# Layer normalisation moved from a block of its own into the block of each cross attention

## The chip, the cores and the metric

The kernel runs on one core of a Trainium2 chip. The core has a matmul engine (TensorE, PE in the rows; PEld is its weight load), VectorE (DVE), ScalarE (ACT), GpSimd (POOL) and SyncE (SP, which issues DMAs). They run independent instruction streams and meet through semaphores. The metric is device time in microseconds (us), the median of several runs; lower is better.

## The reference

Two decoder layers over x, which has 8 batches of 128 tokens with 128 columns, in float32. Each layer is a self attention, a cross attention on a context of 77 rows per batch, and a mixture of experts, each behind a layer normalisation without gain or offset:

```python
x = x + L0_attn(_layernorm(x), ...)
x = x + L0_xattn(_layernorm(x), ctx_768, Wq, bq, Wk, bk, Wv, bv, Wo, bo)
x = x + L0_ffn(_layernorm(x), ...)
x = x + L1_attn(_layernorm(x), ...)
x = x + L1_xattn(_layernorm(x), ctx_768, Wq, bq, Wk, bk, Wv, bv, Wo, bo)
x = x + L1_ffn(_layernorm(x), ...)

def _layernorm(x, eps=1e-05):
    m = mean(x, -1); v = var(x, -1)
    return (x - m) / sqrt(v + eps)

def xattn(x, y, ...):             # 16 heads of 8 columns, 77 keys per batch
    q, k, v = x @ Wq + bq, y @ Wk + bk, y @ Wv + bv
    weights = softmax(einsum('bhqd,bhkd->bhqk', q, k) * 8 ** -0.5)
    return einsum('bhqk,bhkd->bqhd', weights, v) @ Wo + bo
```

## The kernel before

All 1024 tokens stay in on-chip memory for the whole kernel. `x_all` holds the residual stream (partition = token, 8 batches beside one another), `xn_all` its normalised copy, and `xnT_all` the transposed normalised copy (partition = column, 1024 tokens along the free side), which is what the products with weights read.

The program is a chain of stages. Each stage is a block: every engine gets its part of the block, and at its end all engines meet before the next block starts. In order: set-up, attention of layer 0, `layer_norm("n1_")`, `cross_attention(0)`, `mixture0`, `attention1` (which calls `layer_norm("n3_")` inside), `layer_norm("n4_")`, and `mixture1`, which first calls `cross_attention(1, loads)` and then runs its experts. The change touches the norms n1 and n4 and both cross attentions. The first is called the first place here, the second the second place.

`layer_norm` runs in two halves of four batches. VectorE takes the statistics of a half (L165, L168, L170), GpSimd raises the variance to the power -1/2 (L180), and after the statistics of both halves VectorE writes the eight batches of `xn_all` (L173). TensorE transposes each batch into PSUM (L185), and ScalarE copies each half, 128x512, to `xnT_all` (L190). The block ends there.

`cross_attention` starts with the query product: two float32 matmuls of 512 tokens each (L666), one for each half of `xnT_all`, into the two banks `sbk[0]` and `sbk[1]`, and ScalarE takes each out to `q` with the bias (L740). Meanwhile ScalarE loads its table for the exponential (L737), VectorE clears a PSUM bank (L774), and GpSimd adds the output bias to `x_all` (L823), which is first needed when a batch's output is added to `x_all` (L790), seven steps later. TensorE waits for both `q_out` and then starts 16 steps n, two for each batch. A step has four heads in two groups: scores (L688, in `sbk[n % 2]`), row maximum and shift (layer 0: a clamp L782, the maximum L799 on VectorE, the shift L829 on GpSimd; layer 1: L785 and L803 on VectorE), exponential (L769, ScalarE), eight transposes of the probabilities (L722), their copy to `pT` (L764, ScalarE), and sixteen small products with the values (L712). Each engine walks through the steps in a fixed order written out by hand, with lags between the parts. The normalisation for the following mixture is already done inside the steps, batch by batch.

`cross_attention(1, loads)` also has SP issue the loads of the first two experts of the second mixture (L1481 to L1487).

Of the kernel before, what the change touches and what calls it, by code (L numbers as in the profile page):

```python
# [18 lines left out]
ACT = mybir.ActivationFunctionType  # L19
# [3 lines left out]
B = 8  # L23
# [68 lines left out]
def program(nc, a, out, scratch, spread0):  # L92
# [17 lines left out]
    xnT_all = sb("xnT_all", [P, T])  # L110
# [70 lines left out]

    def norm_tensor(pe, n, turned):
        for b in range(B):
            pe.wait_ge(normed, B * n + b + 1)
            pe.transpose(turned[b // 4][:, P * (b % 4):P * (b % 4) + P], xn_all[:, b, :], ident).then_inc(turn_done, 1)  # L185

    def norm_scalar(act, n, turned):
        for j in range(2):
            act.wait_ge(turn_done, B * n + 4 * j + 4)
            act.activation(xnT_all[:, 512 * j:512 * j + 512], turned[j][:, :], ACT.Copy).then_inc(copied, 1)  # L190

    def layer_norm(tag, loads=None):

        with ExitStack() as st:
            _, ps, _ = tools(st, tag)
            turned = [ps(f"turned{j}") for j in range(2)]
            norms[0] += 1
# [24 lines left out]
    def setup_and_bias(bias0, w0):  # L222

        wq, wkv, wo = w0
        with ExitStack() as st:
# [50 lines left out]
            def _(act):  # L276
# [9 lines left out]
                for l in range(2):  # L286
                    for j in range(2):
# [6 lines left out]
                               ACT.Copy).then_inc(bias_out, 1)  # L294
                norm_scalar(act, 0, p_k[2:4])

            @block.tensor
            def _(pe):
# [12 lines left out]
                pe.wait_ge(k_out, 4)  # L311
                norm_tensor(pe, 0, p_k[2:4])

# [298 lines left out]
    def cross_attention(l, loads=None):  # L612
# [5 lines left out]
        with ExitStack() as st:  # L618
# [13 lines left out]
            bk = ps("back", (P, 4 * P))  # L632
            back = bk[:, :].rearrange("p (h c) -> p h c", c=32)
            SPARE = HG * NKV
            names = ("q_done", "q_out", "scores_done", "scores_read", "max_done", "shifted", "exp_done", "turn_done",
# [28 lines left out]
            def _(pe):  # L664
                for j in range(2):
                    pe.matmul(sbk[j][:, 0, :], wqx[l][:, :], xnT_all[:, 512 * j:512 * j + 512], start=True,  # L666
                              stop=True).then_inc(S["q_done"], 1)
                pe.wait_ge(S["q_out"], since["q_out"] + 2)
                pe.wait_ge(S["pv_zeroed"], since["pv_zeroed"] + 1)
                for n in range(2 * SLOTS + 5):  # L670
# [11 lines left out]
                    if n < STEPS:  # L682
                        b = n // 2
                        if n >= 2:
                            pe.wait_ge(S[bank_read], since[bank_read] + n - 1)
                        for u in range(2):
                            at = 32 * (2 * (n % 2) + u)
                            mm = pe.matmul(sbk[n % 2][:, u, 0:HG * NKV], q[at:at + 32, P * b:P * b + P],  # L688
                                           kblk[l][at:at + 32, b, :], start=True, stop=True)
# [46 lines left out]
            def _(act):  # L736
                act.preload_act_table(ACT.Exp)  # L737
                for j in range(2):
                    act.wait_ge(S["q_done"], since["q_done"] + j + 1)
                    act.activation(q[:, 512 * j:512 * j + 512], sbk[j][:, 0, :], ACT.Identity,  # L740
# [31 lines left out]
            @block.vector  # L772
            def _(dve):
                dve.memset(ob[:, :], 0.0).then_inc(S["pv_zeroed"], 1)  # L774
                for n in range(2 * B + 8):
# [45 lines left out]
            @block.gpsimd  # L821
            def _(pool):
                pool.tensor_tensor(x_all[:, :, :], x_all[:, :, :], free(bo, [[0, B], [1, P]]),  # L823
                                   ALU.add).then_inc(S["with_bias"], 1)
# [26 lines left out]
    with ctx:  # L851
        with ExitStack() as early:
# [4 lines left out]
            attention0(bias0, w0)  # L857
        layer_norm("n1_")
        cross_attention(0)
        mixture0(nc, tools, spread0, x_all, xnT_all, consts, tables, we_hi, we_lo, we_split)  # L860
        attention1(nc, a, tools, layer_norm, x_all, xn_all, xnT_all, consts, rows, cols, eps_pow)
        layer_norm("n4_")
        mixture1(nc, a, tools, cross_attention, x_all, xn_all, xnT_all, consts, tables)
# [964 lines left out]
```

## Time and profile before

| what | us |
|---|---|
| median of the three runs shown | 656.82 (656.30, 656.82, 679.62) |
| span of the profiled execution, first to last instruction | 631.4 |

The profile records one execution. Its times are microseconds from the first instruction of the span. The granted clock of TensorE is given as a share of full speed: 1.00 is 2.4 GHz, 0.50 is 1.2 GHz. In a timeline, instructions of a kind on one engine that follow one another closely are merged into one row with their count, so a row with a count gives the start of the first and the length of the whole run; the bracket gives the idle time of the engine ahead of it and who ended it.

### The profile page before, as it was taken

To read this page: it belongs to the slowest core of one execution; us is meant where nothing else is said; L and a number is where in the kernel's file an instruction comes from. 1 tells how busy PE (TensorE), PEld (TensorE's weight loads), DVE (VectorE), ACT (ScalarE), POOL (GpSimd) and SP (SyncE) were. 2 spreads that over 40 slices of the span, in tenths; PEclk is the share of its full clock that TensorE was granted. 3 is DMA by queue.
4 is the path that set the end of the run, shared out by engine and by line. 5 is a ranking of instruction groups with operands and counts; after the bars stand their busy time and mean duration, and the time that the engine had idled before them with its cause. 6 is when DMAs were issued, how large, how long until landed. Compare 5 with 4: busy or idle time off the path is not lost. (4 is left out here: it accounts for less than half of the span.)

```text
span 631.4 us, 9987 instructions
## 1 busy us (share of the span) xinstructions
PE 533.0 (84%) x3281; PEld 413.8 (66%) x3281; DVE 374.3 (59%) x875; ACT 326.1 (52%) x573; POOL 206.7 (33%) x229
## 2 busy tenths in 40 slices
PE   4698999989866998589999699864499967999996
PEld 2488898978853665457887387724266645777774
DVE  3376584756643465356666417765536638788875
ACT  3265454645403566435555326530246636788893
POOL 1688600000013346216655173011200255445510
PEclk9899999999876699789999569978559978899998
DMA  6913100000000000024432100000200001111201
GB/s 182 214 56 88 50 0 0 0 0 1 1 0 1 1 2 1 1 84 134 135 120 66 50 2 2 0 1 1 67 1 1 3 1 34 33 35 42 59 0 33
DMA packets 23412, 23.71 MB, mean 38 GB/s; under 512 B 3358, under 2 KB 17648, under 8 KB 23152
## 3 DMA queue, kind: packets, MB, share of 16 engines
q1 hardware_dynamic: 22528, 22.66, 12.5%
q10 hardware_dynamic: 848, 0.60, 0.3%
q8 instruction: 20, 0.33, 0.2%
q14 instruction: 16, 0.13, 0.1%
HBM read 22.64 MB, written 0.61 MB: 37 GB/s over the span
## 5 line engine op out<-in xcount | busy, mean ns | idle before, releaser
L1775 DVE TENSOR_TENSOR e_h_lo<-e_h,e_h_hi 128x512 fp32r<-128x512 f32 x60 | 50.7, 875 | 15.5 <-ACT e_h_hi L1636 15.4
L1045 POOL TENSOR_TENSOR e_gc<-e_g,e_c 128x512 f32<-128x512 f32 x32 | 42.0, 1314 | 42.0 <-ACT e_g L1028 22.4
L180 POOL TENSOR_TENSOR rstd<-var,eps_pow 128x4 f32<-128x4 f32 x8 | 8.3, 1039 | 134.0 <-DVE var L170 133.9
L722 PE MATMUL x_turn<-consts,x_p 128*77 128x128 f32 x256 | 42.3, 317 | 9.3 <-ACT x_p L769 9.3
L764 ACT ACTIVATE x_pT<-x_turn 77x1024 f32<-77x1024 f32 x32 | 32.6, 1020 | 32.9 <-PE x_turn L722 32.9
L1632 ACT ACTIVATE e_h<-e_h,m_b 128x512 f32<-128x512 f32 x64 | 43.6, 688 | 10.2 <-PE e_h L1534 10.2
L722 PEld LDWEIGHTS x_turn<-consts,x_p 128*77 128x77 f32 x256 | 33.7, 172 | 19.2 <-ACT x_p L769 16.4
L1093 DVE TENSOR_TENSOR e_h_lo<-e_h,e_h_hi 128x512 fp32r<-128x512 f32 x34 | 23.8, 699 | 26.0 <-ACT e_h_hi L1004 26.0
L1004 ACT ACTIVATE e_h_hi<-e_h 128x512 fp32r<-128x512 f32 x34 | 21.5, 632 | 33.9 <-DVE e_h L1087 28.2
L1636 ACT ACTIVATE e_h_hi<-e_h 128x512 fp32r<-128x512 f32 x64 | 38.6, 633 | 0.0
L416 PE MATMUL a_score<-a_kT,a_qz 128*128 128x128 f32 x256 | 34.5, 278 | 2.8 <-DMA rows<-in_L_xattn_bo 2.8
L416 PEld LDWEIGHTS a_score<-a_kT,a_qz 128*128 128x128 f32 x256 | 32.5, 192 | 4.2 <-issue 3.2
L444 PE MATMUL a_pv<-a_v,a_pT 128*128 128x65 f32 x256 | 33.6, 277 | 0.0
L485 ACT ACTIVATE a_qz<-a_fill 64x512 f32<-64x512 f32 x32 | 18.9, 591 | 28.1 <-PE a_fill L395 25.8
L444 PEld LDWEIGHTS a_pv<-a_v,a_pT 128*128 128x128 f32 x256 | 33.2, 201 | 0.3
L546 DVE SCALAR_TENSOR_TENSOR a_s<-a_score,w_bias 128x512 f32<-128x512 f32 x32 | 22.1, 690 | 18.0 <-PE a_score L416 17.7
L1674 POOL TENSOR_TENSOR m_w_hi<-m_w,e_one 128x512 fp32r<-128x512 f32 x16 | 17.5, 1096 | 44.7 <-PE e_y L1534 29.0
L829 POOL TENSOR_TENSOR x_s<-x_s,x_m 128x616 f32<-128x616 f32 x16 | 19.5, 1216 | 31.7 <-DVE x_m L799 31.7
L688 PE MATMUL x_score<-kblk,x_q 32*128 32x308 f32 x128 | 28.5, 561 | 1.6 <-ACT x_q L740 1.6
L515 ACT ACTIVATE a_p<-a_s 128x512 f32<-128x512 f32 x32 | 20.1, 629 | 18.2 <-DVE a_s L552 18.2
L782 DVE TENSOR_SCALAR x_s<-x_score 128x616 f32<-128x616 f32 x16 | 12.8, 799 | 27.2 <-PE x_score L688 26.7
L834 POOL TENSOR_TENSOR rstd<-var,eps_pow 128x1 f32<-128x1 f32 x16 | 9.0, 562 | 58.1 <-DVE var L809 58.1
(275 smaller groups left out, 1448.6 us busy)
## 6 DMA issues: line engine op xcount, KB each, us to landing
e_c<-spread SPq DMA_DIRECT2D x32, 256.0 KB, 3.2
m_w<-in_L_ffn_W SPq DMA_DIRECT2D x16, 256.0 KB, 3.0
a_raw<-in_experts SPq DMA_DIRECT2D x17, 192.0 KB, 2.4
su_reversed<-scratch SPq DMA_DIRECT2D x1, 1024.0 KB, 6.3
w_wkv<-in_L_attn_Wkv SPq DMA_DIRECT2D x1, 1024.0 KB, 8.7
a_pick_f<-in_pick SPq DMA_DIRECT2D x1, 768.0 KB
x_all<-in_x SPq DMA_DIRECT2D x1, 512.0 KB, 5.6
w_wq<-in_L_attn_Wq SPq DMA_DIRECT2D x1, 512.0 KB, 6.6
```

Source lines behind the costliest of these rows:

```text
L416: mm = pe.matmul(sbk[n % 2][:, h, :], qz[:, hg % 2, h, P * b:P * b + P], kT[:, hg % 2, h // 2, P * b:P * b + P], start=True, stop=True)
L444: mm = pe.matmul(ob[g % 2][:, h, 0:DH0 + 1], pT[g % 2][:, h, :], v[:, hg % 2, b, h, :], start=True, stop=True)
L546: dve.scalar_tensor_tensor(out=s[k][:, :, :], in0=sbk[k][:, :, :], scalar=SC, in1=bias0[:, NG * hg:NG * hg + NG, :], op0=ALU.mult, op1=ALU ...
L688: mm = pe.matmul(sbk[n % 2][:, u, 0:HG * NKV], q[at:at + 32, P * b:P * b + P], kblk[l][at:at + 32, b, :], start=True, stop=True)
L722: mm = pe.transpose(tb[0:NKV, u, P * j:P * j + P], p[k % 2][:, u, j, :], ident)
L764: act.activation(pT[k % 2][:, :, :], tb[0:NKV, :, :], ACT.Copy).then_inc(S["turned_out"], 1)
L1004: act.activation(h_hi[u % 2][:, :], h[u % 2][:, :], ACT.Copy).then_inc(S["hi_done"], 1)
L1045: pool.tensor_tensor(gc[k % 2][:, :], g[u % 2][:, :], c[k % NC][:, :], ALU.mult).then_inc(S["weighted"], 1)
L1093: dve.tensor_tensor(h_lo[u % 2][:, :], h[u % 2][:, :], h_hi[u % 2][:, :].bitcast(F32), ALU.subtract).then_inc(S["lo_done"], 1)
L1632: act.activation(h[half][f], hb[f][:, :], ACT.Gelu, bias=b1[j][:, f:f + 1]).then_inc(S["gelu_done"], 1)
L1636: act.activation(h_hi[half][f - 1][:, :], h[half][f - 1], ACT.Copy).then_inc(S["hi_done"], 1)
L1775: dve.tensor_tensor(h_lo[half][f][:, :], h[half][f], h_hi[half][f][:, :].bitcast(F32), ALU.subtract).then_inc(S["lo_done"], 1)
```

## The change

- The two separate blocks `layer_norm("n1_")` and `layer_norm("n4_")` are gone. The normalisation is now the first work of each cross attention's block; its transposes go to the two banks of `tb`, which the steps use later.
- TensorE does, for each half j: four transposes, wait until ScalarE has copied them to `xnT_all`, one query product. ScalarE does, for each half j: copy, then the take-out of the query product with its bias. VectorE and GpSimd run their whole normalisation first and then what the cross attention had.
- ScalarE's table load stands at the head of the block, ahead of the normalisation. SP's loads of the first two experts likewise start with the block.
- TensorE no longer waits for both `q_out` ahead of the steps: step 0 waits for the first, step 1 for the second.
- GpSimd waits until all eight batches are normalised before it adds the output bias to `x_all`.

```diff
--- before.py
+++ after.py
@@ -179,21 +179,21 @@
             pool.wait_ge(mv_done, (B + 2) * n + (HB + 1) * (h + 1))
             pool.tensor_tensor(rstd[:, half], var[:, half], eps_pow[:, half], ALU.pow).then_inc(rstd_done, 1)
 
-    def norm_tensor(pe, n, turned):
-        for b in range(B):
+    def norm_tensor(pe, n, turned, half=None):
+        for b in range(B) if half is None else range(HB * half, HB * half + HB):
             pe.wait_ge(normed, B * n + b + 1)
             pe.transpose(turned[b // 4][:, P * (b % 4):P * (b % 4) + P], xn_all[:, b, :], ident).then_inc(turn_done, 1)
 
-    def norm_scalar(act, n, turned):
-        for j in range(2):
+    def norm_scalar(act, n, turned, half=None):
+        for j in range(2) if half is None else (half,):
             act.wait_ge(turn_done, B * n + 4 * j + 4)
-            act.activation(xnT_all[:, 512 * j:512 * j + 512], turned[j][:, :], ACT.Copy).then_inc(copied, 1)
+            act.activation(xnT_all[:, 512 * j:512 * j + 512], turned[j], ACT.Copy).then_inc(copied, 1)
 
     def layer_norm(tag, loads=None):
 
         with ExitStack() as st:
             _, ps, _ = tools(st, tag)
-            turned = [ps(f"turned{j}") for j in range(2)]
+            turned = [ps(f"turned{j}")[:, :] for j in range(2)]
             norms[0] += 1
             n = norms[0]
             block = st.enter_context(nc.Block())
@@ -292,7 +292,7 @@
                 act.wait_ge(ld_bias, 16)
                 act.activation(bias0[:, :, :], free(reversed0[:, 0, P - 1:P], [[P, H], [-1, P]]),
                                ACT.Copy).then_inc(bias_out, 1)
-                norm_scalar(act, 0, p_k[2:4])
+                norm_scalar(act, 0, [k[:, :] for k in p_k[2:4]])
 
             @block.tensor
             def _(pe):
@@ -309,7 +309,7 @@
                     pe.matmul(p_v[(b // 2) % 2][:, b % 2, :], ctxT[:, NKV * b:NKV * b + NKV], wv[:, :],
                               start=True, stop=True).then_inc(v_mm, 1)
                 pe.wait_ge(k_out, 4)
-                norm_tensor(pe, 0, p_k[2:4])
+                norm_tensor(pe, 0, [k[:, :] for k in p_k[2:4]])
 
             @block.vector
             def _(dve):
@@ -631,6 +631,9 @@
             ob = ps("pv", (P, 4 * P))
             bk = ps("back", (P, 4 * P))
             back = bk[:, :].rearrange("p (h c) -> p h c", c=32)
+            norms[0] += 1
+            norm = norms[0]
+            turned = [tb[:, j, :] for j in range(2)]
             SPARE = HG * NKV
             names = ("q_done", "q_out", "scores_done", "scores_read", "max_done", "shifted", "exp_done", "turn_done",
                      "turned_out", "pv_done", "o_out", "back_done", "recip_done", "normed", "slot_done", "oT_out",
@@ -663,9 +666,10 @@
             @block.tensor
             def _(pe):
                 for j in range(2):
+                    norm_tensor(pe, norm, turned, half=j)
+                    pe.wait_ge(copied, 2 * norm + j + 1)
                     pe.matmul(sbk[j][:, 0, :], wqx[l][:, :], xnT_all[:, 512 * j:512 * j + 512], start=True,
                               stop=True).then_inc(S["q_done"], 1)
-                pe.wait_ge(S["q_out"], since["q_out"] + 2)
                 pe.wait_ge(S["pv_zeroed"], since["pv_zeroed"] + 1)
                 for n in range(2 * SLOTS + 5):
                     b = batch_at(n, 7)
@@ -683,6 +687,8 @@
                         b = n // 2
                         if n >= 2:
                             pe.wait_ge(S[bank_read], since[bank_read] + n - 1)
+                        else:
+                            pe.wait_ge(S["q_out"], since["q_out"] + n + 1)
                         for u in range(2):
                             at = 32 * (2 * (n % 2) + u)
                             mm = pe.matmul(sbk[n % 2][:, u, 0:HG * NKV], q[at:at + 32, P * b:P * b + P],
@@ -736,6 +742,7 @@
             def _(act):
                 act.preload_act_table(ACT.Exp)
                 for j in range(2):
+                    norm_scalar(act, norm, turned, half=j)
                     act.wait_ge(S["q_done"], since["q_done"] + j + 1)
                     act.activation(q[:, 512 * j:512 * j + 512], sbk[j][:, 0, :], ACT.Identity,
                                    bias=cols[:, 3 * l:3 * l + 1]).then_inc(S["q_out"], 1)
@@ -771,6 +778,7 @@
 
             @block.vector
             def _(dve):
+                norm_vector(dve, norm)
                 dve.memset(ob[:, :], 0.0).then_inc(S["pv_zeroed"], 1)
                 for n in range(2 * B + 8):
                     maxima = free(m[n % 2][:, 0, 0:1], [[HG, 2], [1, HG], [0, NKV]])
@@ -820,6 +828,8 @@
 
             @block.gpsimd
             def _(pool):
+                norm_gpsimd(pool, norm)
+                pool.wait_ge(normed, B * (norm + 1))
                 pool.tensor_tensor(x_all[:, :, :], x_all[:, :, :], free(bo, [[0, B], [1, P]]),
                                    ALU.add).then_inc(S["with_bias"], 1)
                 for n in range(2 * B + 8):
@@ -855,11 +865,9 @@
             w0 = (sb0("wq", [P, H * DH0]), sb0("wkv", [P, 2 * H * DH0]), sb0("wo", [P, 8, P]))
             setup_and_bias(bias0, w0)
             attention0(bias0, w0)
-        layer_norm("n1_")
         cross_attention(0)
         mixture0(nc, tools, spread0, x_all, xnT_all, consts, tables, we_hi, we_lo, we_split)
         attention1(nc, a, tools, layer_norm, x_all, xn_all, xnT_all, consts, rows, cols, eps_pow)
-        layer_norm("n4_")
         mixture1(nc, a, tools, cross_attention, x_all, xn_all, xnT_all, consts, tables)
         store()
 
```

## Rows read from the trace of the kernel before

**Rows 1.** The profile's page: span, TensorE's busy time, and its granted clock in 40 slices (tenths).
```profile
span 631.4 us, 9987 instructions
...
PE 533.0 (84%) x3281; PEld 413.8 (66%) x3281; DVE 374.3 (59%) x875; ACT 326.1 (52%) x573; POOL 206.7 (33%) x229
...
PEclk9899999999876699789999569978559978899998
```

**Rows 2.** Timeline, first place: start us, length us, engine, line, operation, count [idle before].
```profile
187.47 2.36 DVE L173 TENSOR_SCALAR xn_all<-x_all,mv,rstd 128x128 f32<-128x128 f32 x8
...
187.86 2.49 PE L185 MATMUL n_turned<-consts,xn_all 128*128 128x128 f32 x8 [4.28 <-DVE xn_all L173]
...
189.14 0.60 ACT L190 ACTIVATE xnT_all<-n_turned 128x512 f32<-128x512 f32 x1 [10.09 <-PE n_turned L185]
190.39 0.60 ACT L190 ACTIVATE xnT_all<-n_turned 128x512 f32<-128x512 f32 x1 [0.66 <-PE n_turned L185]
191.26 1.28 ACT L737 ACT_TABLE_LOAD   x1 [0.27 <-PEq L194]
...
191.28 2.34 POOL L823 TENSOR_TENSOR x_all<-x_all,rows 128x1024 f32<-128x1024 f32 x1 [2.61 <-SPq L618]
191.30 3.42 PE L666 MATMUL x_score<-xnT_all,wqx 128*128 128x512 f32 x4 [0.94 <-PEq L194]
...
194.75 0.69 ACT L740 ACTIVATE x_q<-x_score,cols 128x512 f32<-128x512 f32 x1 [0.68 <-PE x_score L666]
...
195.49 0.80 PE L688 MATMUL x_score<-kblk,x_q 32*128 32x308 f32 x8 [0.78 <-ACT x_q L740]
196.33 0.80 DVE L782 TENSOR_SCALAR x_s<-x_score 128x616 f32<-128x616 f32 x1 [4.40 <-PE x_score L688]
```

**Rows 3.** Timeline, second place, the same columns.
```profile
445.72 2.49 PE L185 MATMUL n_turned<-consts,xn_all 128*128 128x128 f32 x8 [11.83 <-DVE xn_all L173]
...
449.10 0.34 SPq L1481 DMA_DIRECT2D m_w<-in_L_ffn_W  x1
...
449.14 3.75 PE L666 MATMUL x_score<-xnT_all,wqx 128*128 128x512 f32 x4 [0.94 <-PEq L194]
...
451.23 0.69 ACT L740 ACTIVATE x_q<-x_score,cols 128x512 f32<-128x512 f32 x1 [0.84 <-PE x_score L666]
...
452.94 0.69 ACT L740 ACTIVATE x_q<-x_score,cols 128x512 f32<-128x512 f32 x1 [1.02 <-PE x_score L666]
...
453.68 1.41 PE L688 MATMUL x_score<-kblk,x_q 32*128 32x308 f32 x8 [0.78 <-ACT x_q L740]
455.12 0.80 DVE L785 TENSOR_REDUCE x_m<-x_score 128x8 f32<-128x616 f32 x1 [5.34 <-PE x_score L688]
```

**Rows 4.** Busy time by window, first place: window, length, five engines, granted clock, DMA.
```profile
193.00:194.00 1.00, 1.00 (x3) 0.34 (x1) 0.00 (x0) 0.62 (x1) 0.62 (x1) 0.50 0.09 16
...
195.00:196.00 1.00, 0.51 (x8) 0.31 (x8) 0.00 (x0) 0.44 (x1) 0.00 (x0) 1.00 0.00 0
```

**Rows 5.** ScalarE's timeline: copies of transposed probabilities two steps apart, four pairs.
```profile
202.08 1.02 ACT L764 ACTIVATE x_pT<-x_turn 77x1024 f32<-77x1024 f32 x1 [2.08 <-PE x_turn L722]
...
210.51 1.02 ACT L764 ACTIVATE x_pT<-x_turn 77x1024 f32<-77x1024 f32 x1 [1.29 <-PE x_turn L722]
...
236.44 1.02 ACT L764 ACTIVATE x_pT<-x_turn 77x1024 f32<-77x1024 f32 x1 [0.40 <-PE x_turn L722]
...
242.76 1.02 ACT L764 ACTIVATE x_pT<-x_turn 77x1024 f32<-77x1024 f32 x1 [0.40 <-PE x_turn L722]
...
459.58 1.02 ACT L764 ACTIVATE x_pT<-x_turn 77x1024 f32<-77x1024 f32 x1 [2.08 <-PE x_turn L722]
...
468.02 1.02 ACT L764 ACTIVATE x_pT<-x_turn 77x1024 f32<-77x1024 f32 x1 [1.29 <-PE x_turn L722]
...
481.72 1.02 ACT L764 ACTIVATE x_pT<-x_turn 77x1024 f32<-77x1024 f32 x1 [0.40 <-PE x_turn L722]
...
487.49 1.02 ACT L764 ACTIVATE x_pT<-x_turn 77x1024 f32<-77x1024 f32 x1 [0.40 <-PE x_turn L722]
```

## The prediction

> **What bounds the kernel now.** The page comes first: of a span of 631.4 us TensorE is busy for 533.0, and its granted clock is below full speed in many slices [rows 1]. The kernel is a chain of stages, so a change to the two seams is worth what it takes off the path through them and nothing else. The timelines across the seams come next [rows 2, 3]. There the reader is to see a strictly serial path: VectorE writes `xn_all`, TensorE transposes, ScalarE copies, the block ends, TensorE makes two query products, ScalarE takes out the second, TensorE makes the scores, and VectorE reads them. The measure I use is the time from the first transpose to VectorE's first read of scores. All ahead of it is untouched, and from that read on, each step waits for the one before it. It is 196.33 - 187.86 = 8.47 us in the first place [rows 2] and 455.12 - 445.72 = 9.40 us in the second [rows 3].
>
> The two differ for one reason, and the windows show it: in the first place the clock was 0.50 (1.2 GHz) during the query products and 1.00 (2.4 GHz) when the scores ran [rows 4]. So the four records of the products took 3.42 us against 3.75, and the scores were readable after 196.33 - 195.49 = 0.84 us [rows 2] against 455.12 - 453.68 = 1.44 [rows 3]. The 9.40 is therefore this seam at the lower level, and 0.93 us of the first place is a gift of the clock, not of the program.
>
> **What is removed.** (a) One block end. ScalarE's second copy ends at 190.39 + 0.60 = 190.99 and TensorE starts at 191.30 [rows 2]: 0.31 us, of which about 0.05 remains as a plain hand-over (ScalarE ends at 195.44, TensorE starts at 195.49 [rows 2]). (b) The wait of the scores for the second `q_out`: 0.69 + 0.05 us. Step 0 now needs only the first. (c) The table load, 1.28 us, seems to go from the seam, but it was not on the path: it ended at 192.54, before ScalarE's first take-out could begin (that comes 2.09 us after the product starts, from [rows 3]). Worth nothing. In the new place it is covered by VectorE's statistics, since ScalarE has no work before its first copy, 10.09 us idle there [rows 2].
>
> **What is added.** TensorE is in order, and the code puts the second half's transposes behind the first half's query product, and the second product behind a second ScalarE copy. So there are now two trips TensorE, ScalarE, TensorE where there was one, and nothing for TensorE to do in either. What the words of the change promise, query products beside the normalisation, is not there to be had: VectorE has written the last of the eight batches at 187.47 + 2.36 = 189.83 [rows 2], and the first product cannot start before the first copy ends at 189.74. VectorE's part ends as the product begins. The new seam at the lower clock, counted from the first transpose:
>
> - four transposes until ScalarE reads them: 189.14 - 187.86 = 1.28 [rows 2]
> - copy 0.60 and hand-over 0.05: 1.93
> - first product until ScalarE can read it: 451.23 - 449.14 = 2.09 [rows 3]: 4.02
> - four transposes right behind it: 190.39 - 189.14 = 1.25 [rows 2]: 5.27. ScalarE's first take-out, 0.69, lies in this and is over at 4.71
> - copy and hand-over 0.65: 5.92
> - second product, started anew with its weight load: 2.09 again: 8.01. If the weights are in place it is 452.94 - 451.23 = 1.71 [rows 3]: 7.63. I take 2.09, since the weight load stands behind the wait on the same queue
> - scores of step 0 until VectorE reads them: 1.44 if they start when the product is complete (8.01 - 0.05 + 1.44 = 9.40), less if they stream in behind it. The lower bound is the 0.84 of [rows 2] behind the 7.63: 8.42. I take 9.26, near the upper end, as 1.44 is the row at this clock and only its weight load can hide.
>
> So 9.26 (8.42 to 9.40) stands against 9.40: -0.14 us in the second place. What (a) and (b) give, the second copy trip (0.65), the second cold start of a product (0.38) take back. In the first place 9.26 stands against 8.47: +0.79, because I don't expect the clock to rise there.
>
> **Why not.** TensorE's clock rose at the end of an unbroken run of query products, one time of two. The change breaks this run: 2.09 us of product, 1.25 of transposes, 0.65 of idling, 2.09 of product. The transposes do not seem to help: with eight of them just before, the products still ran at 0.50 [rows 2, 4]. The Trainium skill ("TensorE: Matmul & The Clock Gate", "Why this matters for your kernels") asks for matmuls kept back to back to get the full clock, which speaks against this change. The first place agrees with it, having risen in its longest unbroken product run (0.50 to 1.00), and the second does not contradict it. By that rule alone both places would stay at 0.50, which is the +0.79 - 0.14 above; without it they would be at 0.50 and 1.00 as before, and the sum would be twice -0.14.
>
> **Other waits.** GpSimd's bias addition, 2.34 us, now waits for the last of `xn_all`, 189.83, and ends at 192.2; behind it on GpSimd is the first shift, which needs a maximum that VectorE starts on after 196.33 [rows 2]. Slack is over 4 us, so it costs nothing; without that cover it would cost up to 2.34 a place. VectorE clears its bank after the normalisation, with TensorE in transposes and products. Step 1's scores start after the second take-out, some 0.8 us behind those of step 0, and VectorE comes to them after two operations of 0.80 each: covered in either layer. SP's loads of experts move from 449.10 [rows 3] to the start of the block, some 6.5 us earlier; the experts run after the whole cross attention, later than 487.49 [rows 5], so their landing gains nothing, and in the new place they lie beside statistics.
>
> **Sum.** +0.79 - 0.14 = +0.65 us on the span, with bounds -0.05 + -0.98 = -1.03 and +0.93 + 0 = +0.93. The span of the profiled execution goes from 631.4 to 632.1. Between the span and the median of the runs lie 656.82 - 631.4 = 25.4 us, which the change doesn't touch. Predicted: 656.82 + 0.65 = 657.5.
>
> **The rivals.** What the sum can't fix is where in the steps behind the seam the clock rises. Two steps take 8.43 us at the start of layer 0's steps and 6.32 later, 8.44 and 5.77 in layer 1 [rows 5]. A rise two steps later or earlier than now is worth 2.1 us in the first place and 2.7 in the second.
>
> - *Earlier rise.* The seam's work comes spread over more time, or shifted a little, and the clock rises a pair of steps earlier in one place (-2.1 to -2.7) or both (-4.8): 654.8 to 652.7. For: the rise lies among steps of one pattern, so a shift may move it. Against: nothing in the steps becomes denser. Chance 0.12.
> - *Later rise.* The mirror of it, 659.6 to 662.3. For: TensorE enters the steps with more holes behind it. Chance 0.12.
> - *The change brings what its words say.* A product lies beside work that VectorE still has, and 1.71 us of product leave the path in each place: -3.4, about 653.4. Against: the 189.83 above, and TensorE's order. Chance 0.02.
> - *Slower by over 2%.* The clock doesn't rise in the steps at all. From 481.72 on, layer 1 has about four more pairs at 5.77; with those passed before it, some 5.5 pairs at 2.67 more are 14.7 us, and in layer 0 six pairs at 2.11 are 12.7: 657.5 + 27.4 = 684.9. It decides only where both layers stay low for about half of their steps. Against: both rose while the steps ran, with no product of this seam near. Chance 0.03.
>
> **How the numbers follow.** The forecast's own case, 655.8 to 657.8 with half a microsecond of run spread (656.30 against 656.82) on either side, has 0.70; faster by more than 2% through any cause not seen here, 0.01. The range takes the forecast and each clock rival in one place, with the bounds of the sum: 657.5 - 2.7 - 1.0 = 653.8 and 657.5 + 2.7 + 0.3 = 660.5. Two per cent, about what a measurement of this kernel can tell from no change, are 13 us. Faster 0.01, within 2% 0.96, slower 0.03.
>
> **What the profile after would show.** TensorE's order in the seam: four transposes, a hole of about 0.65, product, four transposes, a hole of 0.65, product, scores without a hole. First transpose to VectorE's first read of scores near 9.3 in both places where the clock is 0.50. ScalarE's table load starts with VectorE's statistics. GpSimd's addition begins right after the last `xn_all`. If the distance is under 8 at a clock of 0.50, my step that TensorE's order makes the halves serial is wrong. If the distances are as said but the total moves by more than 2 us, the clock among the steps is the cause, and the spacing of ScalarE's copies there shows it.

## The result and the profile after

The changed kernel took 630.48 us in the median of four runs (626.87, 629.54, 631.42, 660.19) against 656.91 for the kernel before (656.3 to 679.62, four runs). The ratio given with them is 0.958, interval 0.954 to 0.963: faster by 4%. It sets the three shorter runs of the changed kernel against the three shorter ones of the kernel before, 656.3 to 657.0, and the next paragraph says why that is not like against like. The forecast was 657.5, range 653.8 to 660.5. It was wrong, and so was what I took for the time of the kernel before.

A number of this case can't be read without one fact: both kernels have several times. In all runs made here the kernel before lay 11 times of 78 between 629 and 634 us, 58 times between 649 and 661 and 9 times between 676 and 684. The changed kernel lay 9 times of 16 between 625 and 635, 5 times between 652 and 661, and at 671 and 682. Over all of them the medians are 634.7 us (16 runs) and 655.2 (78), a difference of 3%, and the share of runs in the lowest group, 9 of 16 against 11 of 78, differs by far more than chance gives. That three of the first four runs of the changed kernel were in that group, and none of the four of the kernel before, was luck in part. The profile shown of before (span 631.4) is of the lowest group; the profile shown of after, which follows, is of a run of 660.19 us. So the two profiles stand the wrong way round, the faster kernel with the longer span.

The page of the changed kernel, span and granted clock in 40 slices, answering to [rows 1]:

```profile
span 658.4 us, 9965 instructions
...
PEclk9699999999955579689997789696555577799998
```

Each digit is TensorE's granted clock in tenths of full speed; two runs of 5 stand where the cross attentions run. Timeline of the changed kernel, first place (columns as in [rows 2]):

```profile
177.92 1.28 ACT L743 ACT_TABLE_LOAD   x1 [4.81 <-PEq L338]
...
180.87 1.24 PE L185 MATMUL x_turn<-consts,xn_all 128*128 128x128 f32 x4 [4.28 <-DVE xn_all L173]
...
182.80 2.07 PE L671 MATMUL x_score<-xnT_all,wqx 128*128 128x512 f32 x2 [0.69 <-ACT xnT_all L190]
182.91 2.34 POOL L833 TENSOR_TENSOR x_all<-x_all,rows 128x1024 f32<-128x1024 f32 x1 [1.23 <-DVE xn_all L173]
...
184.66 1.06 PE L185 MATMUL x_turn<-consts,xn_all 128*128 128x128 f32 x4
...
186.41 2.07 PE L671 MATMUL x_score<-xnT_all,wqx 128*128 128x512 f32 x2 [0.69 <-ACT xnT_all L190]
...
188.42 2.25 PE L694 MATMUL x_score<-kblk,x_q 32*128 32x308 f32 x8
...
189.86 0.80 DVE L790 TENSOR_SCALAR x_s<-x_score 128x616 f32<-128x616 f32 x1 [6.44 <-PE x_score L694]
```

This is the order that was forecast, with its two holes of 0.69 us. From the first transpose to VectorE's first read of scores it takes 189.86 - 180.87 = 8.99 us; the sum said 9.26, and [rows 2] had 8.47. The second place, answering to [rows 3]:

```profile
451.17 1.24 PE L185 MATMUL x_turn<-consts,xn_all 128*128 128x128 f32 x4 [11.84 <-DVE xn_all L173]
...
453.10 2.07 PE L671 MATMUL x_score<-xnT_all,wqx 128*128 128x512 f32 x2 [0.69 <-ACT xnT_all L190]
...
454.96 1.06 PE L185 MATMUL x_turn<-consts,xn_all 128*128 128x128 f32 x4
...
456.71 1.13 PE L671 MATMUL x_score<-xnT_all,wqx 128*128 128x512 f32 x2 [0.69 <-ACT xnT_all L190]
...
458.60 0.80 DVE L793 TENSOR_REDUCE x_m<-x_score 128x8 f32<-128x616 f32 x1 [4.89 <-PE x_score L694]
...
461.04 1.10 PE L728 MATMUL x_turn<-consts,x_p 128*77 128x128 f32 x8 [1.64 <-ACT x_p L776]
```

Here it takes 7.43 us, against 9.40 in [rows 3] and 9.26 in the sum. The second product takes 1.13 us where the first took 2.07: the clock has risen between them. What becomes of it is seen by window. The columns are the window, its length, TensorE's busy time with the number of its instructions, the granted clock, the DMA share and GB/s:

```profile
453.00:455.00 2.00, 1.90 (x3) 0.50 0.14 37
455.00:457.00 2.00, 1.31 (x6) 0.59 0.00 0
457.00:459.00 2.00, 1.94 (x10) 1.00 0.00 0
459.00:461.00 2.00, 0.40 (x4) 1.00 0.00 0
461.00:463.00 2.00, 1.82 (x12) 1.00 0.00 0
463.00:465.00 2.00, 1.75 (x20) 0.62 0.00 0
465.00:475.00 10.00, 10.00 (x65) 0.50 0.01 2
475.00:495.00 20.00, 20.00 (x127) 0.50 0.00 1
495.00:515.00 20.00, 20.00 (x126) 0.50 0.00 1
515.00:535.00 20.00, 19.32 (x127) 0.50 0.00 1
```

TensorE is at 1.00 through the end of the seam and the first transposes of step 0, falls to 0.50 after the nearly empty window 459 to 461, and then stays at 0.50 for 72 us although it is busy almost without a gap. A TensorE that is 100% busy for 50 us at half its clock is the largest thing in this profile. In the profile of before the same stretch was over at 474, 17 us after the first transposes of probabilities:

```profile
457.55 1.99 PE L722 MATMUL x_turn<-consts,x_p 128*77 128x128 f32 x8 [2.47 <-ACT x_p L769]
```
```profile
472.00:474.00 2.00, 2.00 (x9) 0.50 0.00 0
474.00:476.00 2.00, 2.00 (x28) 0.97 0.00 0
```

ScalarE's copies show what the low clock costs later in the steps, answering to [rows 5]:

```profile
479.62 1.02 ACT L771 ACTIVATE x_pT<-x_turn 77x1024 f32<-77x1024 f32 x1 [1.29 <-PE x_turn L728]
...
489.74 1.02 ACT L771 ACTIVATE x_pT<-x_turn 77x1024 f32<-77x1024 f32 x1 [1.29 <-PE x_turn L728]
```

Two steps take 10.12 us, not the 8.44 of the first steps in [rows 5], since the back transposes and output products have come in, against 5.77 at the higher clock. So a place as a whole takes longer the later the clock rises in it. Its length is counted here from the start of its first transpose to the start of ScalarE's last copy to `xnT_all`, which for the first place of the kernel before is this row (261.54 - 187.86 = 73.7 us):

```profile
261.54 0.28 ACT L751 ACTIVATE xnT_all<-x_back 128x128 f32<-128x128 f32 x1 [1.52 <-PE x_back L701]
```

Read from the timelines in the same way for each profile, in us:

| kernel (span of the profile) | first place | second place |
|---|---|---|
| before (631.4) | 73.7 | 71.6 |
| before, again (680.0) | 96.6 | 97.9 |
| changed (658.4) | 86.1 | 92.9 |
| changed, again (626.0) | 77.9 | 68.5 |
| only the first place changed (639.8) | 86.1 | 74.6 |
| only the second place changed (624.6) | 75.0 | 68.5 |

The two profiles of before differ by 48.6 us in span, and the two places by 22.9 + 26.3 = 49.2. That profile of before, again, has the two long stretches of 5 in its page:

```profile
PEclk9699999999755555689998779795555556799999
```

So the groups of run times are, in the main, the number of places that stay at the low clock: none, one, two. The 86.1 us lie between a short and a long place: there the clock rose 45 us after the first transposes of probabilities. Only the profiled runs show the places; for the others their number is inferred from the time.

### The profile page after: what moved, and what is told of

It reads as the page before. It is cut to its first block and busy times, and to the rows that moved or that the text cites. A ratio compares the mean times of both kernels' runs of the same rounds, so it can differ in the third digit from the quotient of the medians.

```text
span 658.4 us, 9965 instructions
## 1 busy us (share of the span) xinstructions
PE 568.0 (86%) x3281; PEld 434.6 (66%) x3281; DVE 376.1 (57%) x875; ACT 327.2 (50%) x573; POOL 207.4 (32%) x229
## 5 line engine op out<-in xcount | busy, mean ns | idle before, releaser
L728 PE MATMUL x_turn<-consts,x_p 128*77 128x128 f32 x256 | 57.4, 396 | 6.2 <-ACT x_p L776 6.2
L728 PEld LDWEIGHTS x_turn<-consts,x_p 128*77 128x77 f32 x256 | 46.4, 224 | 19.1 <-ACT x_p L776 9.9
L694 PE MATMUL x_score<-kblk,x_q 32*128 32x308 f32 x128 | 39.3, 715 | 0.1
L793 DVE TENSOR_REDUCE x_m<-x_score 128x8 f32<-128x616 f32 x16 | 12.8, 799 | 45.8 <-PE x_score L694 45.8
L444 PE MATMUL a_pv<-a_v,a_pT 128*128 128x65 f32 x256 | 32.1, 269 | 0.0
L444 PEld LDWEIGHTS a_pv<-a_v,a_pT 128*128 128x128 f32 x256 | 31.6, 192 | 0.3
L718 PE MATMUL x_pv<-x_pT,vx 77*9 77x128 f32 x512 | 29.9, 374 | 1.8 <-ACT x_pT L771 1.8
```

Source lines behind the costliest of these rows:

```text
L444: mm = pe.matmul(ob[g % 2][:, h, 0:DH0 + 1], pT[g % 2][:, h, :], v[:, hg % 2, b, h, :], start=True, stop=True)
L718: mm = pe.matmul(ob[32 * j:32 * j + VW, P * hg:P * hg + P], vx[l][:, b, HG * hg + j, :], pT[k % 2][:, u, P * j:P * j + P], start=True, sto ...
L728: mm = pe.transpose(tb[0:NKV, u, P * j:P * j + P], p[k % 2][:, u, j, :], ident)
```

## The experiments

Theory A: the time of a run is set by how long the clock stays at 0.50 in the steps of the two cross attentions, and the change moves the odds of that. Theory B: the change took 25 us of work or waiting off some path. In each experiment "under 640" counts the runs of the lowest group.

**Both kernels again, and each place alone.** The first two are unchanged files. In the others the new parts stand under `if inside:`, with the old block in front of the other place:

```diff
+    INSIDE = (0,)          # or (1,)
+            inside = l in INSIDE
+        if 0 not in INSIDE:
+            layer_norm("n1_")
```

> The kernel before, unchanged, to see a profile and more times of it. Its profiled execution had a span of 631.4 us while its measured times lie at 656 to 657 us, so that profile was not typical. Theory A (clock among the steps): the typical execution has TensorE's granted clock at 0.50 through most of the steps of one or both cross attentions, where two steps take 8.4 us instead of 6.3 (layer 0) or 5.8 (layer 1); 12 to 16 steps at the lower level in both give +25 us, so times near 656 us, and now and then one near 632. Theory B (the seam itself): times at 656 us come from something outside the steps, the steps rise to 1.00 after 15 us as in the first profile, and the difference lies ahead of or behind them.

> The changed kernel, unchanged. Theory A: the seams of both kernels take the same time within 1 us (9.0 us in the profile after), and the times fall into two groups, near 629 us where the clock rises early in both cross attentions and near 660 where it stays at 0.50 for 58 and 72 us as in the profile after; the difference to the kernel before is how often each group comes. Theory B: the times stay near 629 us with a profile whose steps look like those of the kernel before, and 25 us are missing elsewhere.

> Only the first cross attention has its normalisation inside; the second keeps the separate block. Theory A: the clock's rise in a cross attention depends on how its steps lie against the clock, so this kernel takes the low stretch of one cross attention off, or of none: 642 to 657 us, and the profile's granted clock in the steps of each cross attention accounts for the difference within 2 us. Theory B (each place gives its share): about half of the gain, 644 us, with the same clock as before.

> Only the second cross attention has its normalisation inside. Theory A: as with the first only, 642 to 657 us, or 632 where the rise comes early in both; the granted clock among the steps accounts for it. Theory B: about half of the gain, 644 us.

| kernel | median us | range | under 640 |
|---|---|---|---|
| before, again | 652.27 | 629.52 to 681.75 | 1 of 6 |
| changed, again | 643.57 | 625.32 to 681.75 | 6 of 12 |
| only the first place | 655.40 | 639.22 to 660.78 | 1 of 6 |
| only the second place | 641.78 | 626.42 to 674.09 | 6 of 12 |

The ratio of the low groups alone was 0.994, interval 0.982 to 1.006, for the changed kernel, and 0.996, 0.988 to 1.004, for the second place alone. The changed kernel's 9 runs under 640 have a median of 627.8 and the 11 of the kernel before 631.2. So within one group the change is worth some 3 us by these medians, and the intervals don't exclude that it is worth nothing; the rest is the odds: 9 of 16 against 11 of 78. Theory B falls. The gain hangs on the second place: changed alone it gives 6 of 12 against the 11 of 78. The first place alone gives 1 of 6, the odds of the kernel before (a second run, of 641.58 us, is just above the bound). In five profiles of the changed form, two of them of the delayed kernels below, the first place took 86.1, 77.9, 86.1, 78.1 and 75.3 us; in nine of the old form it took 73.7 to 77.6 us seven times and 95.6 and 96.6 twice. No gain shows there.

**The hole behind the scores.** TensorE has nothing to do between the scores of step 1 and the first transposes of probabilities, and the clock that the seam has won is lost behind it. Two products whose result nobody reads fill it:

```diff
+                    if n == 1:
+                        for w in (512, 256):
+                            pe.matmul(tb[:, 1, 0:w], wqx[l][:, :], xnT_all[:, 0:w], start=True, stop=True)
                     k = n - 1
```

and in two kernels all eight transposes go ahead of both products, on TensorE and likewise on ScalarE:

```diff
                 for j in range(2):
                     norm_tensor(pe, norm, turned, half=j)
+                for j in range(2):
                     pe.wait_ge(copied, 2 * norm + j + 1)
```

> The changed kernel with all eight transposes ahead of both query products, and two products whose result nobody uses (512 and 256 tokens) in the hole of TensorE between the scores of step 1 and the first transposes of probabilities. Theory A (the clock in the steps decides): TensorE now works without a hole from the first transpose into the steps, so it enters them at 1.00 and keeps it; the low stretch of both cross attentions goes, every run lies near 615 to 622 us and the spread between runs falls from 50 us to under 10. Theory B (the steps' clock is not set by what comes before them): low stretches of 15 to 70 us stay in the steps, and the runs keep their groups near 626, 652 and 680 us, 3 us lower for the shorter seams.

> The kernel before with the same two unused products in the hole between the scores of step 1 and the first transposes of probabilities; normalisation in its own block. Theory A: one run of TensorE of 3.4 + 1.4 + 2.6 us with a single hole of 0.8 us ahead of the steps is mostly enough to enter them at 1.00; most runs near 620 to 630 us, though without the change. Theory B: as the kernel before, groups near 630, 655 and 678 us, most at 655.

> The changed kernel with only the two unused products added, its halves still one after the other. In three profiles the clock had risen to 1.00 during its second query product at the second place and was given back in the hole behind the scores. Theory A: with the hole filled it is kept, at the second place in nearly all runs, at the first in many: 617 to 640 us, none near 680. Theory B: the same mix as the changed kernel, 9 of 16 runs under 640 and the others up to 682 us.

> The changed kernel with all eight transposes ahead of both query products and nothing else. By the terms of the sum each seam (first transpose to VectorE's read of scores) falls from 9.0 to about 7.3 us at 0.50, less where the clock rises in it: 3.4 us together. Theory A: TensorE's hole of 2.5 to 3.7 us behind the scores is still there, so the clock is given back in it, and the runs keep their groups (near 623, 650 and 677 us) with some mix of them. Theory B (what counts is the seam alone): 3.4 us less than the changed kernel in each group and the same mix.

| kernel | median us | range | first place | second place |
|---|---|---|---|---|
| reordered and filled | 612.97 | 610.70 to 639.33 | 66.2 | 61.8 |
| before, filled | 624.83 | 622.36 to 648.93 | 73.2 | 65.1 |
| changed, filled | 621.38 | 616.19 to 624.76 | 70.2 | 66.7 |
| reordered only | 649.75 | 627.71 to 653.96 | 73.1 | 68.2 |

The kernel before ran at 653.98 beside them. The useless work takes 2.93 us at the low clock, not the 2.6 expected (L723 in the timeline of the changed and filled kernel). It took 9 us off the lowest times of the changed kernel, 625.32 to 616.19, and its upper groups altogether. The old form with the same filling is at 624.8 without anything of the change: four runs at 622 to 625 us, two still at 646 and 649. Its profile has the first transposes of probabilities 11.97 us after the first transpose of the second place, 0.14 us later than without the filling, so there the filling hardly shifts the steps. Their first pair takes 5.62 us instead of 8.44, as TensorE is at 1.00 from the start. Reordering alone shortens the seam, to 6.68 and 6.06 us with the clock rising in it where 7.3 was expected at 0.50, and leaves the odds of the kernel before: 1 of 6. Two of the six runs of the reordered and filled kernel (628.26 and 639.33) lay outside the 615 to 622 us expected, the other four below it, at 610.70 to 613.57. Neither of the two was profiled, so why they are longer stays open. Against the lowest group of the kernel before alone, the lowest groups of the three filled kernels have ratios of 0.969 (0.963 to 0.974), 0.987 (0.981 to 0.993) and 0.983 (0.973 to 0.992), in the order of the table. The windows of the reordered and filled kernel, second place, steps included:

```profile
434.00:439.00 5.00, 4.76 (x11) 0.50 0.41 121
439.00:440.00 1.00, 1.00 (x6) 1.00 0.00 0
440.00:460.00 20.00, 18.48 (x192) 1.00 0.00 1
460.00:480.00 20.00, 19.94 (x221) 1.00 0.01 2
```

The clock rises ahead of the scores and is kept through the steps. In the changed and filled kernel the rise comes within step 0 or 1, behind the filling:

```profile
440.00:452.00 12.00, 11.31 (x28) 0.50 0.02 4
452.00:454.00 2.00, 1.85 (x22) 0.78 0.00 0
454.00:474.00 20.00, 19.02 (x222) 1.00 0.01 2
```

**A pure shift.** If the odds depend on when the steps begin, work that only delays the second place should change them. In the first lines of `norm_vector`, one or two unused additions (a third and fourth write to the halves of `xnT_all`, a fifth operation is a maximum into a small tile of its own):

```diff
+        if n == 3:
+            for h in range(1):        # or 2
+                dve.tensor_tensor(xn_all[:, HB * h:HB * h + HB, :], x_all[:, HB * h:HB * h + HB, :],
+                                  x_all[:, HB * h:HB * h + HB, :], ALU.add)
```

> The kernel before with one unused VectorE addition (128x512, some 0.7 us) ahead of the statistics at the second place, so the whole of what follows comes 0.7 us later with its form unchanged. So far 6 of 41 runs of the kernel before lay under 640 us, 9 of 16 of the changed kernel and 7 of 12 of the kernel with only the second place changed. Theory A1 (it is the moment at which the steps begin against the clock's own timing that decides, and the change only shifted it): the mix of runs moves clearly, to at least 4 in 10 under 640 us, or to none. Theory A2 (it is the form of the new seam, its products and transposes joined, that lets the clock rise there): the mix stays near 1 in 7 under 640 us, most runs near 656, and the profile shows 0.50 through the second place's products.

> The kernel before with two such unused additions, 1.4 us. Theory A1: a third mix, different from that of the kernel before and from that with one addition. Theory A2: the same mix as the kernel before, about 1 in 7 under 640 us, 1.4 us later.

> The changed kernel with the same unused addition of 0.7 us ahead of the statistics at the second place. Theory A1 (the moment decides): the mix of runs moves away from 9 of 16 under 640 us, to 2 in 10 or less, or to nearly all. Theory A2 (the form decides): the mix stays near one half, and the profile shows the clock at 1.00 within the second place's products, as in the three profiles so far.

> The kernel before with three unused additions, about 2.1 us, ahead of the statistics at the second place. The shares under 640 us were 9 of 56 with none, 2 of 6 with 0.7 us, 5 of 6 with 1.4 us. Moment alone: the changed kernel enters the second place's steps about 2.0 us earlier than the kernel before, this one 2.1 us later; if the share rises and falls with the shift it is past its best here or near it, and differs from that of 1.4 us or not, but stays a function of the shift; median between 629 and 655 us. Form alone: back to 1 in 7, median 655 us.

> The changed kernel with two unused additions, about 1.4 us, at the second place, so that its steps there begin about as late as 0.6 us before those of the kernel before. Moment alone: its share under 640 us falls to that of the kernel before with no or little shift, 1 to 2 of 6, median near 652 us. Form alone: it stays at half or more, median near 630 us, as with 0.7 us (5 of 6).

> The kernel before with four unused additions, about 2.8 us, ahead of the statistics at the second place. Moment: the share under 640 us goes on as a function of the shift, between the 6 of 6 at 2.1 us and whatever comes at 3.4. Added work of any length: 5 or 6 of 6 again, median near 633 us.

> The kernel before with four unused additions and one unused maximum, about 3.4 us, ahead of the statistics at the second place. Moment: the clock has come round to where the kernel before meets it, and the share under 640 us is back at 0 to 2 of 6, median near 658 us. Added work of any length: 5 or 6 of 6, median near 634 us.

> The kernel before with one unused addition, 0.7 us, once more. Moment: between the share of the kernel before (1 in 7) and that of 1.4 us (5 of 6), so 1 to 4 of 6. Added work of any length: 5 or 6 of 6, and the 2 of 6 of the first time were chance.

Some counts in these texts are off by one: it was 7 of 41, not 6, and 6 of 12, not 7. An addition moved the seam by 0.60 us rather than 0.7, as TensorE's idle time ahead of the first transpose shows; in order of none [rows 3], one, two, three, four and five operations it grows from 11.83 us so:

```profile
445.85 2.49 PE L189 MATMUL n_turned<-consts,xn_all 128*128 128x128 f32 x8 [12.43 <-DVE xn_all L177]
```
```profile
442.79 2.49 PE L189 MATMUL n_turned<-consts,xn_all 128*128 128x128 f32 x8 [13.04 <-DVE xn_all L177]
```
```profile
441.83 2.49 PE L190 MATMUL n_turned<-consts,xn_all 128*128 128x128 f32 x8 [13.63 <-DVE xn_all L178]
```
```profile
440.99 2.49 PE L191 MATMUL n_turned<-consts,xn_all 128*128 128x128 f32 x8 [14.23 <-DVE xn_all L179]
```
```profile
468.73 2.48 PE L194 MATMUL n_turned<-consts,xn_all 128*128 128x128 f32 x8 [14.83 <-DVE xn_all L182]
```

| form, delay of the second place in us | under 640 | median us | second place in the profile |
|---|---|---|---|
| before, 0 | 11 of 78 | 655.2 | 71.6, 97.9 |
| before, 0.60 (two sets of runs) | 3 of 11 | 653.79, 657.74 | 94.7, 92.9 |
| before, 1.21 | 5 of 6 | 629.76 | 70.7 |
| before, 1.80 | 6 of 6 | 632.87 | 69.7 |
| before, 2.40 | 5 of 6 | 635.87 | 74.7 |
| before, 3.00 | 0 of 7 | 650.00 | 96.0 |
| changed, 0 | 9 of 16 | 630.48, 643.57 | 92.9, 68.5 |
| changed, 0.60 | 5 of 6 | 632.46 | 71.2 |
| changed, 1.21 | 5 of 6 | 636.58 | 71.0 |

One run of 2704.85 us is left out of the 3 of 11; its cause is not known. This is the decisive table. The kernel before, made to do 1.2 us more work and nothing less, has a median of 629.76, level with the changed kernel's 630.48. Its share in the low group goes up (16 of 18 for the delays of 1.21 to 2.40 us) and, at 3.00 us, comes down again. So it is the moment and not the added work, as far as seven runs at 3.00 us show it: four of them lie at 642 to 650 us, between the old groups, and not at the 658 expected. The 2 of 6 of the first set at 0.60 us was neither the 4 in 10 nor the none that theory A1 had asked for. The windows below are of the kernel before with 0.60 and with 1.21 us; both start their steps alike, busy nearly without a gap at 0.50, and one of them is granted the clock at 470 and the other is not for another 58 us.

Delay 0.60:

```profile
457.00:470.00 13.00, 12.92 (x85) 0.50 0.01 1
470.00:472.00 2.00, 2.00 (x11) 0.50 0.00 0
472.00:506.00 34.00, 34.00 (x216) 0.50 0.00 1
```

Delay 1.21:

```profile
453.00:470.00 17.00, 16.09 (x98) 0.50 0.00 1
470.00:472.00 2.00, 2.00 (x29) 0.98 0.00 0
472.00:506.00 34.00, 32.48 (x369) 1.00 0.01 2
```

What stays open: whether a shift is all that the changed kernel's own odds rest on. Its second place reaches the first transposes of probabilities 461.04 - 451.17 = 9.87 us after the first transpose, where the kernel before needs 11.83 (457.55 - 445.72 in its timeline), so it is an advance of 2 us. But with 0.60 and 1.21 us on top it kept 5 of 6, where the moment alone had asked for 1 to 2 of 6 at 1.21. In both profiles both products take 2.07 us, so the clock doesn't rise in the seam, and the first transposes of probabilities come 11.43 us after the first transpose, not 9.87. With the delay these kernels so begin their steps 0.2 and 0.8 us later than the undelayed kernel before (11.43 + 0.60 - 11.83 and 11.43 + 1.21 - 11.83). In the old form the delays move the steps by less than the seam, as the clock rose in three of the seams: the distance is 11.23, 11.12 and 10.86 us with 0.60, 1.21 and 1.80, so its steps begin 0.0, 0.5 and 0.8 us later, with shares of 3 of 11, 5 of 6 and 6 of 6. Counted so, from one profile each, 5 of 6 twice fits the moment alone too; the 9 of 16 of the undelayed changed kernel, 2 us earlier, has no counterpart in the old form. Whether the seam's form has a part in it, or what the changed first place does to the second, no run here separates. And within six runs a share is known only roughly.

**Filling the idle time ahead as well.** Two unused products of 512 tokens at the head of each block, ahead of the transposes, on top of the reordered and filled kernel:

```diff
+                for j in range(2):
+                    pe.matmul(sbk[j][:, 0, :], wqx[l][:, :], xnT_all[:, 512 * j:512 * j + 512], start=True, stop=True)
                 for j in range(2):
                     norm_tensor(pe, norm, turned, half=j)
```

> The kernel with reordered halves and the hole filled behind the scores (it ran at 610.7 to 613.6 us four times, 628 and 639 once each), and in addition two unused products of 512 tokens on TensorE at the head of each cross attention's block, while VectorE takes the statistics. They lie in TensorE's idle time there (4.3 and 3.4 us). Theory A: TensorE enters the steps at 1.00 in every run, the two outliers go, and the seams run at 1.00 more often: 606 to 612 us for all. Theory B: the outliers have another cause (the other stages): they stay, one run in three over 620 us.

Median 614.46, range 608.35 to 617.56, beside 655.90 for the kernel before. The two outliers are gone, as theory A said, but only one run of six lies within its 606 to 612 us. The places took 65.3 and 60.5 us, the shortest of all. The spread is 9 us instead of 50. The median isn't below the 612.97 of the kernel without the second filling, but no run is above 618. Either kernel beats both the kernel before and the changed one, by 6% and some 3% of their medians.

## Why the prediction was wrong, point by point

- *The sum against the median.* The step "between the span and the median lie 25.4 us, which the change doesn't touch" failed first. A run takes 1.8 us more than its own span (660.19 us with a span of 658.4). The rest of the 25.4 us was no overhead. It was one cross attention at 0.50 in the timed runs and not in the profiled one: the two profiles of runs of 656.80 and 657.16 us (the kernel before with the delay of 0.60) have a first place of 77.6 and 73.8 us and a second of 94.7 and 92.9. And the change does touch it: the share of runs without it went from 11 of 78 to 9 of 16. The profile shown was not of the case that the median described, and this gap was the sign.
- *The seam.* Its order, the two holes, the extra hand-over, the covered table load (177.92, with the statistics), GpSimd's addition right behind `xn_all` (182.91) and its slack were as said. 9.26 against 8.99 in the first place: the second transposes came 1.86 us after the first product began (184.66 - 182.80) and not 2.09, they and the copy took 1.75 us (186.41 - 184.66) and not 1.90, and product and scores took 0.11 more than their 3.34. In the second place it was 7.43, as the clock rose, a case that I had excluded from the bounds (8.42 to 9.40).
- *"The change breaks the run of products, so the clock won't rise."* Wrong at the second place. In three profiles (the changed kernel twice and the second place alone) the second product there ran in 1.12 to 1.13 us, behind a stretch of product and transposes joined; the 3.75 us of products alone of [rows 3] had not raised it. The old form can do it too: with the delays of 1.21 and 1.80 us its products at the second place ended at the higher clock (seams of 8.68 and 8.42 us instead of 9.40). So the break in the run of products doesn't decide it. I had read the rows as if transposes counted for nothing, and the rule of the Trainium skill ("TensorE: Matmul & The Clock Gate", "Why this matters for your kernels") on back-to-back work as if it were about the products alone. The filled kernels agree with that rule as the page states it; the 72 us of a busy TensorE at 0.50 do not, and there the measurement decides.
- *The clock in the steps.* The right cause, with far too small a price. I let the rise come two steps earlier or later (4.8 us), and gave 3 in 100 to the case that it does not come at all (27.4 us). It was the commonest case: as far as their times tell, 67 of the 78 runs of the kernel before had it in one place or both. Its size was off as well: 22.9 and 26.3 us for a place (96.6 - 73.7, 97.9 - 71.6) where I had 12.7 and 14.7, because a pair of late steps at 0.50 takes 10.12 us and not 8.44.
- *The sign.* The rival "earlier rise", 0.12, was the right way but priced from one profile, which already was near the earliest case (the shortest second place of the unfilled kernels is 68.2 us, against its 71.6). Little was left there to gain; nearly all of it was in the runs that the profile did not show.

## What to carry to other kernels

Before a sum is made against a profile, ask which of the timed runs the profile could be: a gap between its span and the median that is larger than the usual couple of microseconds means that the profile shows another case, and the sum then needs the price and odds of each case. Where an engine is 100% busy at half its clock, look at the first idle hole ahead of that stretch, not at the stretch: 2.9 us of useless products in such a hole were worth far more here (medians of 613 to 625 us against 654) than the seam that was tuned (some 3 us, not clear of noise). And a change whose gain is far above its sum should be tried against a plain delay in the same place before it is believed.

## What the runs showed of the hardware that I had not expected

- TensorE's granted clock can stay at 0.50 for 72 us of steps in which TensorE is busy nearly all the time (the windows 465 to 535 above), in narrow transposes and products. Where the clock rose among these steps it was kept through nearly all the rest of the place (from 474 to 512 us in the profile of before, whose place ends at 517); the rise ahead of them, at 457 in the profile of after, was lost at 463.
- Whether it rises early depends, at the second place of the old form, on the moment at which they begin: 11 of 78, 3 of 11, 5 of 6, 6 of 6, 5 of 6 and 0 of 7 runs in the low group for delays of 0, 0.60, 1.21, 1.80, 2.40 and 3.00 us.
- Runs of the kernel before, on one core at a time, lay up to 55 us apart (628.93 to 683.88 us) over all sets and 52 us within one set (631.56 to 683.88), with the mean granted clock between 0.89 and 0.80.
